# The inverse blocks of a chunked delta rule: U and T loaded together, the way out in two halves, and new orders of the steps

## The chip, the cores and the metric

One Trainium2 chip, of which the kernel uses one core. The metric is device time in microseconds (us) for one launch. Everything is float32. The names of the engines are those of the profile: PE is the matrix engine (PEld its loads of weights), DVE the vector engine, ACT the scalar engine, POOL the GpSimd engine, and SP the queue that issues nearly all transfers (DMAs).

## The reference, cut to what matters

A layer normalisation feeds two branches that are added to the input: a gated delta rule (linear attention with 32 heads of 64, 4 sequences of 256 tokens) and a small gated feed-forward part (1024 wide, with Walsh-Hadamard transforms). The change lies in the delta rule.

```
xn = layernorm(x)
q, k, v, z = split(xn @ w_qkvz.T)
q, k, v = causal depthwise convolution of 4 taps
g = -exp(A_log) * softplus(a + dt_bias); beta = sigmoid(b)
q = l2norm(q) / 8; k = l2norm(k)
for t in range(256):
    S = S * exp(g_t)
    delta = (v_t - k_t @ S) * beta_t
    S = S + outer(k_t, delta)
    o_t = q_t @ S
out = (rmsnorm(o) * norm_weight * sigmoid(z)) @ w_out.T
y = x + out + ffn(xn)
```

## The kernel before, in words

The loop over tokens is replaced by chunks of 64 tokens. Within a chunk the deltas solve a triangular system of 64 by 64, so the kernel forms the Gram matrix of the keys (gram, L779), scales it (ATP, L309), and inverts the triangle. A step of the kernel handles one pair of heads m (16 pairs, `PAIRS`), and for it 16 units (4 sequences by 4 chunks), with the two heads of a pair on the two halves of the 128 partitions.

The inverse is made in two stages.

- The base: the 4 diagonal blocks of 16 by 16 of each of the 32 triangles are carried to one row per block. `bout` (L641) writes the blocks of ATP to the DRAM scratch `base_blocks`, 8 DMAs of 16 KB; `bin_` (L647) reads them back as 128 rows of 256 numbers into `UU[:, 0]`; DVE inverts all 128 blocks at once in 16 small instructions (`inv` with i of 0, 1, 2, L338 to L360); ACT writes the transposed blocks into `UU[:, 1]` (L1090); `uout` (L653) writes both to the scratch `inverse_blocks`, and `uin` (L665 to L668) brings them back to where the matmuls want them: the blocks U to `U16` (8 DMAs), the transposed T to `T16` (6 DMAs), and the first block column to `X` (2 DMAs). Each of these 16 DMAs has 16 partitions by 16 units by 16 numbers, 16 KB.
- The rest of the triangle: `hz` on PE with j of 0 to 3 (L802, L804, L806), where ACT turns the first product into Q (L1099), and DVE adds U to the products (`hz` on DVE, L371).

Behind it stands the serial part of the pair, per chunk c: `delta` (L835, d copied by ACT at L1105), `state` (L848, added by DVE at L387), `ks` (L818, added by DVE at L376), then the outputs `o` (L863), their norm and gate, and `out` (L915, L421). Beside all this run the projections of later pairs (`proj`, L715 on PE, L1043 on ACT, L259 on DVE, the costliest lines), the norms of the keys (`stats`), the feed-forward part (`ff`, `fo`), and POOL's scalings.

Each engine works through a list of steps that is written out by hand as text ("0.hz.1.0" is pair 0, step hz, j of 1, half 0); the engines meet only in semaphores. An engine therefore waits at the head of its own list, whatever stands behind. On SP one list orders `load` (weights of the projection, 512 KB, L599), `rload` (decay rows, 6 DMAs, L614 and L617), `fload`, `oload` (128 KB, L632), `bout`, `bin`, `uout` and `uin`. `uout` waits for ACT's transposition (`ut_done`), `uin` for `uout` to land, and PE's `hz` of j 0 for all of `uin` (`ui_in` at 16 times `UIN`). `UIN` counts the DMAs.

```
uin waits: uu_out, then issues 16 DMAs (UIN = 16 * 16)
hz, j = 0, on PE: pe.wait_ge(ui_in, (m + 1) * UIN)
```

Of the kernel before, what the change touches and what calls it, by code (L numbers as in the profile page):

```python
# [89 lines left out]
def layer(nc, sem, sb, ps, k, cst, xnT, beta, yacc, xh, wdf, coef, x, wqkvz, wba, conv, alog, dtb, nw, wout,  # L90
          su_ug, su_dp, ws_up, ws_gate, ws_dp, wgu, wdown, consts, drows, dblk, dub):

    with ExitStack() as ctx:
# [153 lines left out]
        with nc.Block() as block:  # L247
            @block.vector
            def _(dve):
# [266 lines left out]
                for n in (15, 13, 11, 9, 7, 5, 3, 1):  # L516
# [20 lines left out]
                         "state": state, "norm": norm, "gated": gated, "turn": turn, "out": out, "fold": fold, "fo": fo}, """0.fold 0.proj.0 0.proj.1 0.proj.2 0.proj.3 0.e 0.proj.4 0.stats 0.proj.5 0.gram.0 0.gram.1 1.e 0.ff 0.gram.2 0.gram.3  # L537
                     1.proj.0 1.proj.1 0.fo.0 1.proj.2 1.proj.3 0.inv.0 1.proj.4 1.stats 1.proj.5 1.ff 1.gram.0 1.gram.1 0.inv.1 0.fo.1
                     0.inv.2 1.gram.2 1.gram.3 0.vtr.0 1.fo.0 2.ff 0.vtr.1 2.proj.0 2.e 1.fo.1 2.fo.0 3.ff 2.proj.1 2.fo.1 2.proj.2
                     0.hz.1.0 3.fo.0 0.hz.1.1 1.inv.0 0.hz.2.0 0.hz.2.1 3.fo.1 0.hz.3.0 0.hz.3.1 1.inv.1 2.proj.3 0.state.0 0.ks.1 2.proj.4  # L540
                     0.state.1 0.ks.2 0.norm.0 1.inv.2 0.state.2 0.gated.0 0.ks.3 2.stats 2.proj.5 0.norm.1 0.turn.0 2.gram.0 2.gram.1
                     0.gated.1 0.out.0 2.gram.2 0.turn.1 0.out.1 1.vtr.0 0.out.2 0.out.3 1.vtr.1 2.gram.3 3.proj.0 3.proj.1 3.e 1.hz.1.0
                     1.hz.1.1 2.inv.0 1.hz.2.0 1.hz.2.1 3.proj.2 1.hz.3.0 1.hz.3.1 3.proj.3 1.state.0 2.inv.1 1.ks.1 3.proj.4 1.state.1
                     1.ks.2 1.norm.0 2.inv.2 1.state.2 1.gated.0 1.ks.3 3.stats 3.proj.5 1.norm.1 1.turn.0 3.gram.0 3.gram.1 1.gated.1
                     1.out.0 1.turn.1 1.out.1 3.gram.2 3.gram.3 1.out.2 1.out.3 2.vtr.0 2.vtr.1 4.proj.0 4.proj.1 2.hz.1.0 2.hz.1.1
                     2.hz.2.0 2.hz.2.1 2.hz.3.0 2.hz.3.1 3.inv.0 4.e 2.state.0 3.inv.1 2.ks.1 4.proj.2 2.state.1 4.proj.3 2.ks.2 2.norm.0
                     4.proj.4 2.state.2 2.gated.0 2.ks.3 3.inv.2 2.turn.0 2.norm.1 4.proj.5 2.gated.1 2.out.0 2.turn.1 2.out.1 4.stats
                     3.vtr.0 2.out.2 4.gram.0 4.gram.1 2.out.3 4.ff 3.vtr.1 4.gram.2 3.hz.1.0 3.hz.1.1 4.gram.3 3.hz.2.0 3.hz.2.1 5.e
                     3.hz.3.0 3.hz.3.1 5.proj.0 5.proj.1 3.state.0 4.inv.0 3.ks.1 4.inv.1 3.state.1 5.proj.2 3.ks.2 3.norm.0 5.proj.3
                     3.gated.0 3.state.2 5.proj.4 3.ks.3 4.inv.2 3.turn.0 3.norm.1 5.proj.5 3.gated.1 3.out.0 3.turn.1 3.out.1 5.stats  # L550
                     4.vtr.0 5.gram.0 3.out.2 3.out.3 5.gram.1 5.ff 4.vtr.1 5.gram.2 5.gram.3 4.hz.1.0 4.hz.1.1 4.hz.2.0 4.hz.2.1 6.e
                     4.hz.3.0 4.hz.3.1 6.proj.0 6.proj.1 4.state.0 5.inv.0 4.ks.1 5.inv.1 4.state.1 6.proj.2 4.ks.2 6.proj.3 4.norm.0
                     4.state.2 6.proj.4 4.ks.3 4.gated.0 5.inv.2 4.turn.0 4.norm.1 6.proj.5 4.out.0 4.gated.1 4.turn.1 6.stats 5.vtr.0
                     6.gram.0 4.out.1 4.out.2 4.out.3 6.gram.1 6.ff 5.vtr.1 6.gram.2 5.hz.1.0 5.hz.1.1 6.gram.3 5.hz.2.0 5.hz.2.1 7.e
                     5.hz.3.0 5.hz.3.1 7.proj.0 7.proj.1 5.state.0 6.inv.0 5.ks.1 6.inv.1 5.state.1 7.proj.2 5.ks.2 5.norm.0 7.proj.3
                     5.gated.0 5.state.2 7.proj.4 5.ks.3 6.inv.2 5.turn.0 5.norm.1 7.proj.5 5.out.0 5.gated.1 5.turn.1 7.stats 6.vtr.0
                     7.gram.0 5.out.1 5.out.2 7.gram.1 5.out.3 7.ff 6.vtr.1 7.gram.2 7.gram.3 6.hz.1.0 6.hz.1.1 6.hz.2.0 6.hz.2.1 8.e
                     6.hz.3.0 6.hz.3.1 8.proj.0 8.proj.1 6.state.0 7.inv.0 6.ks.1 7.inv.1 6.state.1 8.proj.2 6.ks.2 6.norm.0 8.proj.3
                     6.state.2 8.proj.4 6.ks.3 6.gated.0 7.inv.2 6.turn.0 6.norm.1 8.proj.5 6.gated.1 6.turn.1 6.out.0 6.out.1 8.stats
                     7.vtr.0 6.out.2 8.gram.0 6.out.3 8.gram.1 7.vtr.1 8.ff 8.gram.2 8.gram.3 7.hz.1.0 7.hz.1.1 7.hz.2.0 7.hz.2.1 9.e  # L560
                     7.hz.3.0 7.hz.3.1 9.proj.0 9.proj.1 7.state.0 8.inv.0 7.ks.1 8.inv.1 7.state.1 9.proj.2 7.ks.2 9.proj.3 7.norm.0
                     7.state.2 9.proj.4 7.ks.3 7.gated.0 8.inv.2 7.turn.0 7.norm.1 9.proj.5 7.out.0 7.gated.1 7.turn.1 9.stats 8.vtr.0
                     9.gram.0 7.out.1 9.gram.1 7.out.2 7.out.3 9.ff 8.vtr.1 9.gram.2 9.gram.3 8.hz.1.0 8.hz.1.1 8.hz.2.0 8.hz.2.1 10.e
                     8.hz.3.0 8.hz.3.1 10.proj.0 10.proj.1 8.state.0 9.inv.0 8.ks.1 9.inv.1 8.state.1 10.proj.2 8.ks.2 10.proj.3 8.norm.0
                     8.state.2 10.proj.4 8.ks.3 8.gated.0 9.inv.2 8.turn.0 8.norm.1 10.proj.5 8.gated.1 8.out.0 8.turn.1 10.stats 10.gram.0
# [743 lines left out]
```

## Time and profile before

| | |
|---|---|
| median of 3 runs | 844.16 us (843.19 to 848.38) |
| the profiled execution's own time | 839.25 us |
| its span, first to last instruction | 837.5 us |
| outside the span | 1.75 us |
| granted PE clock, mean over the span | 0.974 of full |
| instructions in the span | 27042 |

The durations of the prediction come from the profiled execution, whose time lies 4.9 us under the median of the three runs. A busy share of an engine is its busy time over the span; matmuls are pipelined, so a busy PE need not be at its peak. A row of a timeline gives the start, the time it took (of all instructions merged into the row) and, in brackets, how long the engine was idle before it and who ended that.

### The profile page before, as it was taken

What the parts mean: (1) busy time and instruction counts of PE and PEld (TensorE: products, weight loads), DVE (VectorE), ACT (ScalarE), POOL (GpSimd) and SP (SyncE); (2) the same over time, 40 slices, a digit from 0 to 9 for tenths busy, and PEclk for the clock granted to TensorE, in tenths of its full rate; (3) what the DMA queues carried; (4) which work ended last, traced back from release to release, by engine and by line L of the source; (5) the groups of instructions that cost most, each with busy time, mean ns of one, the idle gap of its engine ahead of it and who ended that gap; (6) DMA issues with size and microseconds to landing.
All of it is one profiled execution on the core that took longest, in us unless ns stands there. A gap on an engine that the chain in (4) does not pass through costs nothing.

```text
span 837.5 us, 27042 instructions
## 1 busy us (share of the span) xinstructions
PE 743.5 (89%) x11562; PEld 490.0 (59%) x11562; DVE 688.2 (82%) x1224; ACT 326.3 (39%) x737; POOL 278.0 (33%) x186
## 2 busy tenths in 40 slices
PE   1869997989899989999999999999988898989986
PEld 1534554655666656755666566666565565656674
DVE  4688995988789879878989989898897888896645
ACT  2234432525353526343443535253634335353210
POOL 3025321605243241525133323426061523242301
PEclk9979998999999999999999999999999999999989
DMA  7122230321414050312314040413113140302201
...
DMA packets 131703, 49.28 MB, mean 59 GB/s; under 512 B 111488, under 2 KB 121088, under 8 KB 131456
## 3 DMA queue, kind: packets, MB, share of 16 engines
...
## 4 chain that ended last, share of the span: by engine, by line
PE 48%; DVE 15%; SPq 14%; DMA 10%; issue 7%; ACT 4%; POOL 2%; DVEq 0%; ACTq 0%; POOLq 0%
PE bank L715 15%; SPq L641 4%; PE bank L863 4%; PE bank L835 4%; SPq L665 4%; DVE kq L259 3%; DMA UU<-base_blocks 3%; PE bank L743 3%; PE bank L736 3%; SPq L667 3%; PE bank L806 3%; PE bank L915 2%; DMA inverse_blocks<-UU 2%; DMA base_blocks<-ATP 2%; PE bank L848 2%
## 5 line engine op out<-in xcount | busy, mean ns | idle before, releaser
L715 PE MATMUL bank<-xnT,wq 128*128 128x512 f32 x512 | 254.4, 622 | 1.3 <-DVE kq L259 1.1
L259 DVE SCALAR_TENSOR_TENSOR kq<-bank,cw,kq 128x510 f32<-128x510 f32 (+2 forms) x288 | 213.6, 745 | 17.9 <-ACT kq L1043 11.0
L715 PEld LDWEIGHTS bank<-xnT,wq 128*128 128x128 f32 x512 | 90.8, 194 | 83.4 <-issue 72.1
L1043 ACT ACTIVATE kq<-bank,cw 128x512 f32<-128x512 f32 x96 | 65.8, 687 | 174.8 <-PE bank L715 146.6
L1231 POOL TENSOR_TENSOR Sd<-St,dec 128x256 f32<-128x256 f32 x32 | 22.6, 706 | 276.5 <-DVE St L383 224.0
L1235 POOL TENSOR_TENSOR ost<-ost,cst 128x8 f32<-128x8 f32 x32 | 53.8, 1680 | 134.1 <-DVE ost L396 134.0
L1225 POOL TENSOR_TENSOR kqg<-kq,rows 128x1024 f32<-128x1024 f32 x32 | 77.4, 2438 | 41.9 <-DVE kq L259 41.9
L915 PE MATMUL bank<-wo,oT 128*128 128x256 f32 x256 | 68.2, 384 | 0.0
L1195 POOL TENSOR_TENSOR stat<-stat,cst 128x16 f32<-128x16 f32 x16 | 46.3, 2896 | 39.8 <-DVE nV L318 39.8
L736 PE MATMUL bank<-xh,wguT 128*128 128x512 f32 x128 | 57.9, 595 | 0.0
L371 DVE TENSOR_TENSOR X<-U,bank 128x256 f32<-128x256 f32 (+1 forms) x96 | 42.8, 460 | 17.9 <-PE bank L804 8.2
L915 PEld LDWEIGHTS bank<-wo,oT 128*128 128x128 f32 x256 | 45.8, 190 | 16.6 <-issue 10.8
L806 PE MATMUL bank<-X,Q 64*32 64x32 f32 x2048 | 41.4, 195 | 14.2 <-DVE X L371 10.4
L1105 ACT ACTIVATE d<-bank 128x256 f32<-128x256 f32 x64 | 24.5, 383 | 75.5 <-PE bank L835 75.3
L1074 ACT ACTIVATE vt<-bank 64x256 f32<-64x256 f32 x128 | 48.3, 377 | 9.6 <-PE bank L743 5.5
L806 PEld LDWEIGHTS bank<-X,Q 64*32 64x32 f32 x2048 | 36.6, 111 | 25.1 <-DVE X L371 14.3
L1203 POOL TENSOR_TENSOR gb<-E,stat 128x512 f32<-128x512 f32 x32 | 35.4, 1126 | 46.7 <-issue 27.1
L421 DVE TENSOR_TENSOR yacc<-yacc,bank 128x512 f32<-128x512 f32 x64 | 42.9, 680 | 9.7 <-PE bank L917 4.9
L1065 ACT ACTIVATE kc<-bank 64x256 f32<-64x256 f32 x128 | 48.2, 377 | 4.4 <-PE bank L743 1.2
L1047 ACT ACTIVATE zt<-bank 128x512 f32<-128x512 f32 x32 | 17.6, 595 | 75.7 <-DVE oT L409 69.0
L309 DVE TENSOR_TENSOR ATP<-bank,gb 128x512 f32<-128x512 f32 x64 | 42.4, 683 | 5.1 <-PE bank L779 2.9
L743 PE MATMUL bank<-cst,kq 128*128 128x128 f32 x256 | 41.0, 289 | 1.8 <-DVE ATP L309 1.8
...
## 6 DMA issues: line engine op xcount, KB each, us to landing
...
rows<-decay_rows SPq DMA_DIRECT2D x32, 256.0 KB, 4.3
inverse_blocks<-UU SPq DMA_DIRECT2D x16, 256.0 KB, 2.0
wguT<-wgu_dram SPq DMA_DIRECT2D x8, 256.0 KB, 4.1
...
base_blocks<-ATP SPq DMA_DIRECT2D x128, 16.0 KB, 1.8
...
```

The costliest lines, as they stand in the source:

```text
L259: nc.vector.scalar_tensor_tensor(out=y[:, :, t:S], in0=p[:, :, 0:S - t], scalar=cw[:, m, i // 2, 3 - t:4 - t], in1=y[:, :, t:S], op0=ALU.m ...
L715: last = nc.tensor.matmul(ring[i % 2][:], wq[:, q, kc, i // 2, :], xnT[:, kc, (i % 2) * 512:(i % 2) * 512 + 512], start=kc == 0, stop=kc = ...
L736: last = nc.tensor.matmul(ff_bank(m, j)[:], wguT[:, j, kc, :], xh[:, kc].rearrange("p (b t c) -> p b t c", b=B, t=2)[:, :, q, :], start=kc ...
L743: last = nc.tensor.transpose(TG[H][:, i * P:i * P + P], kq[:, which, 2 * H + i // 2, i % 2 * P:i % 2 * P + P], k("ident"))
L806: last = nc.tensor.matmul(M[H][top[h], i * n + n - H2:i * n + n], Q[hs[h], u, 0:H2], X[hs[h], q, u, H2:C], start=True, stop=True)
L915: last = nc.tensor.matmul(dst, oT[:, t, b, :], wo[:, q, :], start=True, stop=not ffn)
L1043: nc.scalar.activation(kq[:, i // 2, 2 * (i % 2):2 * (i % 2) + 2, :], split(ring[i % 2][:], 2), ACT.Copy, scale=cw[:, m, i // 2, 3:4]).the ...
L1065: nc.scalar.activation(kc_[place(h, H), H * HALF + c:H * HALF + HALF:2], split(TG[H][hs[c], :], 4)[:, :, h * C:h * C + C], ACT.Copy).then_ ...
L1074: nc.scalar.activation(vt[place(h, H), H * HALF + c:H * HALF + HALF:2], split(TG[H][hs[c], :], 4)[:, :, h * C:h * C + C], ACT.Copy).then_i ...
L1195: nc.gpsimd.tensor_tensor(stat[:, 2], stat[:, 5], k("half"), ALU.pow).then_inc(root_done, 1)
L1225: nc.gpsimd.tensor_tensor(kqg[:, q, :, half(H)].rearrange("p k u c -> p k (u c)"), src, g, ALU.mult).then_inc(kqg_done, 1)
L1235: nc.gpsimd.tensor_tensor(ost[:, 2, :], ost[:, 1, :], k("neghalf")[:, 0:B * 2], ALU.pow).then_inc(rms_done, 1)
```

## The change

U16 and T16 become the two halves of one tile `UT`, and `inverse_blocks` is laid out with the kind (U or T) ahead of the unit. Then one DMA brings a block of U and of T for all 16 units: 8 DMAs of 16 partitions by 32 by 16 numbers (32 KB) in place of 14 of 16 KB, with the 2 for X as they were, 10 DMAs for a pair in place of 16. The T block of the last block row, which before was not loaded, comes along. `uout` is issued as two DMAs of 128 KB: the half with U as soon as DVE has inverted (`inv_step`), the half with T when ACT has transposed. One memset on POOL in place of two. The lists of all five engines are written anew; the counts of steps in them are the same (657, 116, 755, 418 and 176 for DVE, SP, PE, ACT and POOL).

```
-        U16 = tmp("U16", [UNITS, C])
-        T16 = tmp("T16", [UNITS, C])
+        UT = tmp("UT", [2, UNITS, C])
+        U16, T16 = UT[:, 0], UT[:, 1]
...
-        UIN = 16 * 16
+        UIN = 16 * 10
...
                 def bin_(m, q):
                     sp.wait_ge(at_out, (m + 1) * 2 * NB * 16)
-                    wait(sp, uu_out, m * 16)
+                    wait(sp, uu_out, m * 32)
                     sp.dma_start(UU[:, 0], dblk.rearrange("h i u r c -> (h i u) (r c)")).then_inc(nb_in, 16)
                 def uout(m, q):
-                    sp.wait_ge(ut_done, m + 1)
                     wait(sp, ui_in, m * UIN)
-                    sp.dma_start(dub.rearrange("h i u k r c -> (h i u) (k r c)"), UU[:].rearrange("p k f -> p (k f)")).then_inc(uu_out, 16)
+                    sp.wait_ge(inv_step, (m + 1) * NINV)
+                    for i in range(2):
+                        if i:
+                            sp.wait_ge(ut_done, m + 1)
+                        sp.dma_start(dub[:, :, i].rearrange("h i u r c -> (h i) u (r c)"), UU[:, i]).then_inc(uu_out, 16)
                 def uin(m, q):
-                    sp.wait_ge(uu_out, (m + 1) * 16)
+                    sp.wait_ge(uu_out, (m + 1) * 32)
...
                     for h in range(2):
                         for i in range(NB):
                             at, cols = h * C + i * BASE, slice(i * BASE, i * BASE + BASE)
-                            sp.dma_start(U16[at:at + BASE, :, cols], dub[h, i, :, 0].rearrange("u r c -> r u c")).then_inc(ui_in, 16)
-                            if i < NB - 1:
-                                sp.dma_start(T16[at:at + BASE, :, cols], dub[h, i, :, 1].rearrange("u r c -> r u c")).then_inc(ui_in, 16)
-                        sp.dma_start(X[h * C:h * C + BASE, q, :, 0:BASE], dub[h, 0, :, 0].rearrange("u r c -> r u c")).then_inc(ui_in, 16)
+                            sp.dma_start(UT[at:at + BASE].rearrange("p k u c -> p (k u) c")[:, :, cols], dub[h, i].rearrange("k u r c -> r (k u) c")).then_inc(ui_in, 16)
+                        sp.dma_start(X[h * C:h * C + BASE, q, :, 0:BASE], dub[h, 0, 0].rearrange("u r c -> r u c")).then_inc(ui_in, 16)
...
-                ("inverse_blocks", (2, C // BASE, UNITS, 2, BASE, BASE)))]
+                ("inverse_blocks", (2, C // BASE, 2, UNITS, BASE, BASE)))]
```

Of the lists two lines, from DVE's:

```
-                     0.hz.1.0 3.fo.0 0.hz.1.1 1.inv.0 0.hz.2.0 0.hz.2.1 3.fo.1 0.hz.3.0 0.hz.3.1 1.inv.1 2.proj.3 0.state.0 0.ks.1 2.proj.4
+                     0.hz.1.1 3.fo.0 0.hz.2.0 0.hz.2.1 1.inv.0 3.fo.1 0.hz.3.0 0.hz.3.1 1.inv.1 2.proj.3 0.state.0 0.ks.1 2.proj.4
```

SP, from the second half of pair 0's loads of the inverse blocks to pair 1's way into UU. Before:

```order
L665 DMA U<-inverse_blocks 16x16x16
L667 DMA T<-inverse_blocks 16x16x16
L665 DMA U<-inverse_blocks 16x16x16
L668 DMA X<-inverse_blocks 16x16x16
L632 DMA woraw<-wout_dram 128x256
L641 DMA base_blocks<-ATP 16x16x16 x8
L599 DMA wq<-wqkvz_dram 128x1024
L647 DMA UU<-base_blocks 128x256
```

Now, from the way out of pair 0 on (L656 is `uout`, L668 the loads of UT, L669 those of X):

```order
L656 DMA inverse_blocks<-UU 8x16x256 x2
L632 DMA woraw<-wout_dram 128x256
L668 DMA UT<-inverse_blocks 16x32x16 x4
L669 DMA X<-inverse_blocks 16x16x16
L668 DMA UT<-inverse_blocks 16x32x16 x4
L669 DMA X<-inverse_blocks 16x16x16
L641 DMA base_blocks<-ATP 16x16x16 x8
L599 DMA wq<-wqkvz_dram 128x1024
L647 DMA UU<-base_blocks 128x256
```

A pair now has 10 of these loads and not 16, and the load of the output weights (L632) moved from behind them into the wait for the way out. The load of the projection's weights still stands ahead of L647.

DVE, in pair 0's `hz` (L371), where the base inverse of pair 1 begins (L338, which waits for L647's DMA). Before:

```order
L371 TENSOR_TENSOR X<-U,bank 128x8x48
L439 TENSOR_TENSOR yacc<-yacc,bank 128x2x256
L371 TENSOR_TENSOR X<-U,bank 128x8x48
L338 MEMSET UU 128x16
L340 TENSOR_TENSOR prod<-UU 128x8
L341 TENSOR_TENSOR UU<-UU,prod 128x4x2
L342 TENSOR_TENSOR prod<-UU 128x8
L343 TENSOR_TENSOR UU<-UU,prod 128x4x2
L371 TENSOR_TENSOR X<-U,bank 128x8x32 x2
L439 TENSOR_TENSOR yacc<-yacc,bank 128x2x256
L371 TENSOR_TENSOR X<-U,bank 128x8x32 x2
```

Now:

```order
L371 TENSOR_TENSOR X<-UT,bank 128x8x48 x2
L439 TENSOR_TENSOR yacc<-yacc,bank 128x2x256
L371 TENSOR_TENSOR X<-UT,bank 128x8x32 x2
L338 MEMSET UU 128x16
L340 TENSOR_TENSOR prod<-UU 128x8
L341 TENSOR_TENSOR UU<-UU,prod 128x4x2
L342 TENSOR_TENSOR prod<-UU 128x8
L343 TENSOR_TENSOR UU<-UU,prod 128x4x2
L439 TENSOR_TENSOR yacc<-yacc,bank 128x2x256
L371 TENSOR_TENSOR X<-UT,bank 128x8x32 x2
```

The first instruction of the base inverse, and the wait in front of it, moved from behind the two additions of j 1 to behind the two of j 2.

DVE, the same place in pair 11 (base inverse of pair 12). Before:

```order
L371 TENSOR_TENSOR X<-U,bank 128x8x48 x2
L371 TENSOR_TENSOR X<-U,bank 128x8x32
L338 MEMSET UU 128x16
L340 TENSOR_TENSOR prod<-UU 128x8
L341 TENSOR_TENSOR UU<-UU,prod 128x4x2
```

Now:

```order
L371 TENSOR_TENSOR X<-UT,bank 128x8x48 x2
L371 TENSOR_TENSOR X<-UT,bank 128x8x32 x4
L338 MEMSET UU 128x16
L340 TENSOR_TENSOR prod<-UU 128x8
L341 TENSOR_TENSOR UU<-UU,prod 128x4x2
```

Here it moved behind all six additions of the pair. In pairs 1 and 13 it moved as in pair 0, in pair 14 behind all six as in pair 11; in pairs 3 to 9 it stands in the same place in both lists, behind the first addition of `state`. On SP the 512 KB `load` of a later pair stands between `bout` and `bin` in pairs 1 and 6 before, and in pairs 0, 1, 4, 6, 7, 9, 10, 11, 12 and 13 now.

## Rows read from the trace of the kernel before

**Rows 1.** The page's busy time by engine (PE, DVE), and its last chain

```profile
PE 743.5 (89%) x11562; PEld 490.0 (59%) x11562; DVE 688.2 (82%) x1224; ACT 326.3 (39%) x737; POOL 278.0 (33%) x186
...
PE 48%; DVE 15%; SPq 14%; DMA 10%; issue 7%; ACT 4%; POOL 2%; DVEq 0%; ACTq 0%; POOLq 0%
```

**Rows 2.** Busy time by stretch: length, PE, PEld, DVE, ACT, POOL, clock, DMA share, GB/s

```profile
0.00:118.70 118.70, 85.81 (x522) 46.90 (x522) 93.64 (x149) 43.02 (x95) 35.46 (x24) 0.96 0.34 92
118.70:254.80 136.10, 120.00 (x2024) 80.00 (x2024) 110.66 (x205) 53.49 (x123) 45.31 (x30) 0.95 0.24 50
254.80:627.90 373.10, 356.63 (x5724) 235.84 (x5724) 327.47 (x583) 159.41 (x359) 135.29 (x90) 0.99 0.26 58
627.90:760.90 133.00, 117.23 (x2090) 79.97 (x2090) 113.53 (x208) 53.89 (x124) 50.09 (x34) 0.99 0.26 57
760.90:837.50 76.60, 63.84 (x1204) 47.26 (x1204) 42.86 (x85) 16.53 (x40) 11.84 (x9) 0.94 0.13 31
```

**Rows 3.** Who waited for whom: us in total, times, longest

```profile
DVE UU L338 <- DMA UU<-base_blocks: 18.7, 8, 5.5
...
PE bank L806 <- DVE X L371: 10.4, 7, 5.3
...
PE bank L802 <- DMA X<-inverse_blocks: 2.1, 4, 0.6
```

**Rows 4.** Timeline of SP, pair 0 to 1: start, us, instruction

```profile
109.18 0.33 SPq L665 DMA_DIRECT2D U<-inverse_blocks  x1
...
116.43 0.45 SPq L668 DMA_DIRECT2D X<-inverse_blocks  x1
...
117.46 6.61 SPq L641 DMA_DIRECT2D base_blocks<-ATP  x8
...
125.47 0.34 SPq L647 DMA_DIRECT2D UU<-base_blocks  x1
```

**Rows 5.** Timelines of DVE and PE at the same place

```profile
130.10 0.07 DVE L338 MEMSET UU<- 128x16 f32 x1 [5.49 <-DMA UU<-base_blocks]
...
124.87 1.20 PE L806 MATMUL bank<-X,Q 64*32 64x32 f32 x64
131.37 1.86 PE L806 MATMUL bank<-X,Q 64*32 64x32 f32 x62 [5.29 <-DVE X L371]
```

**Rows 6.** Stretches, columns as rows 2: behind the stall of pair 0, and two later ones

```profile
131.37:135.40 4.03, 4.03 (x67) 2.93 (x68) 3.19 (x10) 0.00 (x0) 0.00 (x0) 0.50 0.00 0
180.00:184.00 4.00, 3.98 (x38) 2.79 (x39) 3.16 (x6) 0.38 (x1) 0.62 (x1) 0.57 0.01 4
368.00:372.00 4.00, 3.92 (x83) 3.27 (x83) 3.49 (x9) 0.60 (x1) 1.62 (x2) 0.59 0.02 4
```

**Rows 7.** Timeline of SP: issues of DMAs with many rows

```profile
0.74 1.00 SPq L672 DMA_DIRECT2D xs<-x_dram  x2
1.79 0.89 SPq L674 DMA_DIRECT2D cst<-consts_dram  x1
...
17.76 0.43 SPq L685 DMA_DIRECT2D yacc<-x_dram  x1
```

**Rows 8.** One stretch of loads of the inverse blocks alone, columns as rows 2

```profile
480.00:488.00 8.00, 7.99 (x32) 5.29 (x31) 6.50 (x11) 1.77 (x3) 6.71 (x5) 1.00 0.31 30
```

**Rows 9.** Timelines of SP, DVE and PE, pair 11

```profile
626.57 5.15 SPq L641 DMA_DIRECT2D base_blocks<-ATP  x8
...
636.49 0.07 DVE L338 MEMSET UU<- 128x16 f32 x1 [3.12 <-DMA UU<-base_blocks]
...
642.73 0.68 PE L835 MATMUL bank<-nV,X 64*64 64x64 f32 x16 [2.23 <-issue]
```

**Rows 10.** Timeline of PE, pair 15: its first product with T

```profile
798.40 2.07 PE L802 MATMUL bank<-T,ATP 64*64 64x48 f32 x64
```

**Rows 11.** The page's DMA issues: count, KB each, us to landing

```profile
inverse_blocks<-UU SPq DMA_DIRECT2D x16, 256.0 KB, 2.0
```

**Rows 12.** The chain in order of time: `bin` behind a 512 KB load, and alone

```profile
361.04 4.43 DMA UU<-base_blocks
...
455.36 2.10 DMA UU<-base_blocks
```

More of the change, by code:

```diff
@@ L543, in _ @@
[L543 to L546, printed above, removed]
@@ L551, in _ @@
[L551 to L554, printed above, removed]
+                     0.gated.1 0.out.0 2.gram.2 0.turn.1 0.out.1 1.vtr.0 2.gram.3 0.out.2 1.vtr.1 0.out.3 3.proj.0 3.proj.1 1.hz.1.0 3.e
@@ new lines, in _ @@
+                program({"load": load, "rload": rload, "fload": fload, "oload": oload, "bout": bout, "bin": bin_, "uout": uout, "uin": uin}, """0.rload 1.rload 0.bout 2.load 0.bin 2.fload 2.rload 0.uout 1.oload 0.uin 1.bout 3.load 1.bin 1.uout 2.oload 1.uin
+                     3.rload 2.bout 2.bin 4.load 2.uout 2.uin 3.bout 4.rload 3.bin 4.fload 5.load 3.uout 3.uin 3.oload 5.rload 4.bout
+                     6.load 4.oload 4.bin 4.uout 4.uin 6.rload 5.bout 5.bin 6.fload 7.load 5.uout 5.oload 5.uin 7.rload 6.bout 8.load 6.bin
+                     6.uout 6.oload 6.uin 8.rload 7.bout 9.load 8.fload 7.bin 7.oload 7.uout 7.uin 9.rload 8.bout 8.bin 10.load 8.uout
+                     8.uin 8.oload 10.rload 9.bout 10.fload 11.load 9.bin 9.uout 9.uin 11.rload 10.bout 12.load 9.oload 10.bin 10.uout
+                     10.uin 12.rload 10.oload 11.bout 13.load 11.bin 11.oload 11.uout 11.uin 12.bout 14.load 12.bin 13.rload 12.oload
+                     12.uout 12.uin 13.bout 15.load 12.fload 13.bin 13.oload 14.rload 13.uout 13.uin 15.rload 14.bout 14.bin 14.oload
+                     14.uout 14.uin 15.bout 15.bin 15.oload 14.fload 15.uout 15.uin""")
@@ L968, in _ @@
                 program({"decays": decays, "proj": proj, "ff": ff, "ktr": ktr, "vtr": vtr, "qsq": qsq, "gram": gram, "hz": hz, "ks": ks, "delta": delta,
-                         "state": state, "o": o, "turn": turn, "out": out, "wd": wd, "fo": fo}, """0.proj.0 0.proj.1 0.decays 0.wd.0 0.proj.2 0.ktr.0 0.proj.3 0.wd.1 0.proj.4 0.ktr.1 0.proj.5 0.ff 0.gram.0 0.proj.6
-                     0.proj.7 0.gram.1 1.proj.0 0.fo.0 1.proj.1 0.vtr.0 0.vtr.1 1.proj.2 0.qsq 1.proj.3 1.ktr.0 0.fo.1 1.ktr.1 1.proj.4
@@ L991, in _ @@
-                     7.proj.5 5.ks.3 7.ktr.1 5.delta.3 5.turn.0 5.o.1.0 5.o.1.1 5.o.1.2 7.proj.6 5.out.0 7.gram.0 7.proj.7 5.turn.1 5.out.1
-                     5.out.2 7.ff 5.out.3 6.hz.0.0 6.hz.0.1 7.gram.1 6.hz.1.0 6.hz.1.1 6.hz.2.0 6.hz.2.1 8.proj.0 6.hz.3.0 6.hz.3.1
+                         "state": state, "o": o, "turn": turn, "out": out, "wd": wd, "fo": fo}, """0.decays 0.proj.0 0.proj.1 0.wd.0 0.proj.2 0.ktr.0 0.proj.3 0.wd.1 0.ktr.1 0.proj.4 0.proj.5 0.ff 0.proj.6 0.gram.0
+                     0.proj.7 0.gram.1 1.proj.0 0.vtr.0 0.fo.0 1.proj.1 0.qsq 1.proj.2 0.vtr.1 1.proj.3 1.ktr.0 0.fo.1 1.proj.4 1.ktr.1
@@ L1029, in _ @@
+                     13.fo.1 14.out.2 14.out.3 15.hz.0.0 15.hz.0.1 15.hz.1.0 15.hz.1.1 15.hz.2.0 15.hz.2.1 15.hz.3.0 15.hz.3.1 15.delta.0
+                     15.state.0 15.ks.1 15.delta.1 15.state.1 15.o.0.0 15.ks.2 15.o.0.1 15.o.0.2 15.delta.2 15.state.2 15.ff 15.ks.3
+                     15.delta.3 15.turn.0 15.o.1.0 15.o.1.1 15.o.1.2 14.fo.0 14.fo.1 15.out.0 15.fo.0 15.fo.1 15.turn.1 15.out.1 15.out.2
+                     15.out.3""")
             @block.scalar
@@ L1189, in _ @@
+                     15.delta.3 15.ff 15.norm.1""")
             @block.gpsimd
```

287 lines of the change are left out of this document (141 added, 146 removed).

## The prediction

> **What bounds the kernel now.** I read the page's busy times first, then the chain, then the stretches, the waits, and last the timelines of single pairs. PE is busy 89% of the span and DVE 82%, and the chain that ended last is 48% PE, 14% issues on SP and 10% DMAs [rows 1]. Averages hide where that holds. By stretches [rows 2], PE is idle for 32.9 us of the first 118.7 us (the prologue, in which PE has nothing to do), for 16.1 us of the stretch of pairs 0 to 2 (136.1 less 120.0), for 16.5 us of the 373 us of pairs 3 to 10 (so PE is 96% busy there), for 15.8 us of pairs 11 to 13, and for 12.8 us of the tail. The whole idle time of PE behind the prologue is 61 us, and half of it lies where only a third of the pairs are. In the middle nothing that is not PE work can give more than some 2 us a pair.
>
> What ends the idle times? PE waited for the loads of the inverse blocks only 2.1 us in total, four times [rows 3]. So the direct effect of faster loads, PE starting its first product sooner, is small in the old list. The larger item is indirect: DVE waited 18.7 us, 8 times, for the DMA into UU (base inverse of the next pair), and PE 10.4 us for DVE's additions to X [rows 3]. The two are one thing. In pair 0, SP issues the 16 loads from 109.18 to 116.88 us, only then the way out of pair 1's blocks (117.46), and the DMA into UU at 125.47 [rows 4]. DVE stands at the head of its list with the base inverse, between the additions of j 1 and those of j 2, and waits 5.49 us; PE, which needs these additions, waits 5.29 us [rows 5]. Behind it the granted clock is 0.50 for the next 4.03 us, the lower of its two levels (1.2 GHz, not 2.4), and after two later stalls 0.57 and 0.59 over 4 us [rows 6]. A stall of PE is thus paid twice. Pair 11 repeats it: bout issued at 626.57 right behind the loads, DVE idle for 3.12 us, PE for 2.23 us [rows 9].
>
> **The loads.** Six DMAs fewer for each pair. Sixteen issues take 7.7 us, 0.48 each [rows 4], so ten take 4.8: 2.9 us less on SP for each pair, if an issue costs the same with 512 pieces of 64 bytes as with 256. No row shows such a DMA. From below: two loads of 512 rows of 1 KB were issued in 1.00 us together, and one of 1024 rows in 0.43 [rows 7], so pieces cost SP nothing. From above: the load right behind those two took 0.89 [rows 7], as if the queue had been full, and then 512 pieces cost 0.98, the ten issues 8 x 0.97 + 2 x 0.48 = 8.7 us, 1.0 more than now. The DMA engines do not decide: they are 0.31 busy in a stretch of these loads [rows 8], that is 8.0 x 16 x 0.31 = 40 engine-us for some 4100 pieces, 9.7 ns each; the new loads have 4608 pieces, 45 engine-us, 2.8 us of all 16, in 4.8 us. I take the fixed cost, as nearer to most rows: 2.9 us less, and 0.1 more to land.
>
> The Trainium skill (DMA: Bandwidth & Descriptors, section Bandwidth, Measured) gives about 10.5 ns for a small packet and calls transfers under 64 KB dominated by descriptors. The measured 9.7 ns agrees. Read as a rule for the whole DMA it speaks against the change, since the bytes are the same and the descriptors 12% more: by it the loads would take no less than before and the term above would be nothing.
>
> **The way out.** One DMA of 256 KB lands 2.0 us after its issue [rows 11]. Now the half with T, 128 KB, is issued at the same point, behind ACT's transposition, and the other ahead. It lands no later than 2.0 and, smaller, perhaps 0.3 sooner; the second issue can cost 0.3. I take nothing, with 1 us to either side of it. The load of the output weights moves into this wait in pairs 0 and 1 and some later ones, which takes another 0.5 us from between loads and bout.
>
> The same page (section on why a DMA increments its semaphore by 16) says that a DMA runs on the largest number of engines up to 16 that divides the outer dimension of both sides. The DRAM side of a half now has 8 there: 8 engines, 16 KB each, as before with 16 and twice the bytes. By that the landing stays 2.0, or more if both halves share the 8 engines in flight. No row here shows a DMA on 8 engines.
>
> **The stalls.** Here the lists and SP's shorter queue work together. Pair 0: bout starts 2.9 + 0.5 = 3.4 us sooner, so UU lands 3.4 us sooner, and DVE's wait stands behind the additions of j 2, so that PE can go on with two products of j 3 (1.2 us each, [rows 5]) and the projection behind them. Of 5.3 us I take 4.8 as gone, and 2.0 for the clock, since 4.03 us at half speed hold 2.0 us of work at full [rows 6]. Together 6.8 us. What is late next is DVE's own list, 110.7 us busy of 136.1 [rows 2], so not at once. Pair 11: the wait now stands behind all six additions, and PE's 2.2 us go. The other six waits are 18.7 - 5.5 - 3.1 = 10.1 us of DVE. By pair 0 nearly all of such a wait can reach PE, by [rows 2] in the middle little does; I take a third, 3.4 us, and for the clock one of the two later dips, 4 - 4 x 0.58 = 1.7 us. Sum of the gains: 6.8 + 2.2 + 3.4 + 1.7 = 14.1 us.
>
> **What it gives back.** The 512 KB load now stands ahead of bin in eight more pairs. Behind such a load UU landed 4.43 us after its issue, alone after 2.10 [rows 12]: 2.3 us later. Where bin comes sooner by 3 us that is covered, but in pairs where bout waited for ATP and not for SP it is not. I take a quarter of 8 x 2.3 = 18.6 us, 4.6 us. In pairs 3 to 9 the first product with T stands at the same place in PE's list as before, so sooner data find PE at other work: nothing. In pair 15 PE came to it without idling [rows 10]: nothing in the tail. The list in the prologue puts the decays ahead of the first projections, where PE idles anyway; nothing, or 2 us either way for the clock.
>
> **Sum.** 839.25 (the profiled execution: span 837.5 and 1.75 around it) - 14.1 + 4.6 = 829.7, so 9.5 us less. The median of the runs lies 4.9 us above the profiled one; 844.16 - 9.5 = 834.7, and I round the half microsecond that the first wait of PE for loads may add: 834.0 us. The forecast's own range is 827 to 839: the gain from 5 to 17 us.
>
> **Rivals.** A: the gain is hidden. For it: PE in the middle is 96% busy, and its other waits (for d, for Y, for St) are serial steps of a pair that no load shortens; when the stall at DVE goes, the same work waits there. Against: the stall of pair 0 is larger than any of those. Then only pair 0's own 5.3 us come through, less the 4.6 given back, 0 to 4 us: 842.
>
> B: pieces cost SP as much as issues do. For it: 0.89 behind the two loads of 512 rows [rows 7]. Against: 0.43 for 1024 rows. The loads then take 1.0 us more in each pair, under lists that no longer have spare work there; before, the first product started within a microsecond of the landing (it waited 4 times). 16 x 1.0 less what little slack there is, with 2.3 us for bin in eight pairs against only half the gains: +16 + 4.6 - 7 = +13.6, near 857. It decides once an issue of 512 pieces takes more than about 0.75 us.
>
> C: the 512 KB load ahead of bin isn't covered. The full 18.6 us in place of 4.6: 844.2 - 14.1 + 18.6 = 848.6, and a half-speed dip behind each of four of them, 1.7 each: 855. For it: 4.43 against 2.10. Against: base inverses stand five or more DVE steps behind, and in pairs 11, 12 and 14 they moved further back. It decides when DVE waits more than 25 us in total for UU.
>
> **How the numbers follow.** Forecast 0.54, A 0.28, B 0.08, C 0.10. A measurement of this kernel tells about 1% (8.4 us, 835.7) from no change. Of the forecast's share I put 0.44 beyond that and 0.10 within; A is within; B and C together 0.14 slower and 0.04 within. So faster 0.44, same 0.42, slower 0.14. The range reaches from 823, all gains and more of the early idle time, to 851, half of the slow cases.
>
> **What would show it.** Right: issues of UT near 0.48 us, SP done with a pair's loads in about 5 us; no wait of PE for X over 2 us near 125 to 135 us, and a clock near 1.0 there; the stretch up to pair 3's first product shorter by 7 or more us; the sum of DVE's waits for UU under 12 us; the stretch of pairs 3 to 10 within 3 us of 373. Wrong: issues of 0.9 us (B); waits of DVE for UU above 20 us, each behind a 512 KB load (C); the first stretch no shorter (A); or the middle stretch changed by more than 5 us, which nothing above explains.

## The result, and the profile after

The changed kernel took 814.53 us (median of 4 runs, 812.68 to 817.35), the kernel before 845.19 us beside it (4 runs, 843.19 to 848.38): a ratio of 0.9637, 95% interval 0.9593 to 0.968. That is 31 us less, where 10 were forecast, and 8.5 us below the low end of the range. The direction was right, the size was not.

The profiled execution has a span of 815.2 us, 22.3 less than the 837.5 of before. The page's busy times and its last chain, to be set beside [rows 1]:

```profile
PE 742.0 (91%) x11562; PEld 485.2 (60%) x11562; DVE 694.7 (85%) x1224; ACT 326.5 (40%) x737; POOL 278.8 (34%) x185
...
PE 54%; DVE 30%; issue 7%; ACT 4%; POOL 3%; DMA 1%; SPq 1%; DVEq 0%; ACTq 0%; POOLq 0%
```

PE has 1.5 us less to do and DVE 6.5 more; of the 22.3 us, 20.8 are idle time of PE that went. SP and the DMAs held 24% of the chain before and hold 2% now, and DVE's share went from 15% to 30%. The stretches, cut at the first product of pairs 0, 3, 11 and 14 as in [rows 2], with the same columns, show where:

```profile
0.00:117.90 117.90, 87.21 (x522) 47.92 (x522) 94.58 (x149) 43.01 (x94) 32.67 (x23) 0.96 0.35 93
117.90:241.30 123.40, 115.30 (x2030) 76.74 (x2028) 111.73 (x203) 52.47 (x121) 45.14 (x31) 1.00 0.28 59
241.30:608.80 367.50, 355.18 (x5721) 232.90 (x5720) 332.12 (x583) 159.53 (x354) 138.19 (x90) 1.00 0.27 59
608.80:738.10 129.30, 118.71 (x2093) 79.58 (x2092) 112.73 (x208) 53.57 (x125) 49.92 (x33) 0.99 0.27 59
738.10:815.20 77.10, 65.64 (x1204) 48.08 (x1204) 43.49 (x85) 17.88 (x43) 12.88 (x10) 0.91 0.14 31
```

Against the five lengths of before the differences are -0.8, -12.7, -5.6, -3.7 and +0.5 us. More than half of the gain is in pairs 0 to 2, where PE's idle time fell from 16.1 to 8.1 us and the granted clock rose from 0.95 to 1.00. Behind the prologue PE idles for 42.5 us in all (8.1 + 12.3 + 10.6 + 11.5), 18.7 less than before. The waits of [rows 3], and one on SP:

```profile
DVE UU L338 <- DMA UU<-base_blocks: 0.3, 1, 0.3
...
PE bank L807 <- DVE X L371: 0.5, 2, 0.3
...
PE bank L803 <- DMA X<-inverse_blocks: 0.5, 1, 0.5
...
SPq L641 <- DVE ATP L309: 48.8, 11, 6.4
```

DVE's wait for UU, 18.7 us before, has gone but for 0.3 us, and with it PE's wait for the additions, 10.4 before and 0.5 now. The last row is the other side: SP stands at `bout` and waits for ATP in 11 pairs, so in 5 of 16 alone `bout` comes straight behind other work of SP. In the trace of before those were 8. SP was the late one, and is less so. SP's timeline at the place of [rows 4]:

```profile
105.46 1.33 SPq L656 DMA_DIRECT2D inverse_blocks<-UU  x2
106.83 0.46 SPq L632 DMA_DIRECT2D woraw<-wout_dram  x1
109.38 3.44 SPq L668 DMA_DIRECT2D UT<-inverse_blocks  x4
112.86 0.49 SPq L669 DMA_DIRECT2D X<-inverse_blocks  x1
113.39 2.03 SPq L668 DMA_DIRECT2D UT<-inverse_blocks  x4
115.46 0.49 SPq L669 DMA_DIRECT2D X<-inverse_blocks  x1
116.05 3.83 SPq L641 DMA_DIRECT2D base_blocks<-ATP  x8
...
121.28 0.33 SPq L647 DMA_DIRECT2D UU<-base_blocks  x1
```

The DMA into UU is issued at 121.28, not 125.47. That is 11.9 us behind the first load of the blocks (109.38), where it was 16.3 (109.18). DVE and PE at the place of [rows 5]:

```profile
125.09 0.07 DVE L338 MEMSET UU<- 128x16 f32 x1 [0.31 <-DMA UU<-base_blocks]
```

```profile
123.11 1.20 PE L807 MATMUL bank<-X,Q 64*32 64x32 f32 x64
124.24 1.13 PE L943 MATMUL bank<-wdf,hf 128*128 128x256 f32 x4
125.30 1.20 PE L807 MATMUL bank<-X,Q 64*32 64x32 f32 x64
126.43 1.98 PE L716 MATMUL bank<-xnT,wq 128*128 128x512 f32 x4
```

DVE waited 0.31 us for 5.49, and PE runs through where it stood for 5.29. From pair 0's first product to pair 1's it is 39.8 us, where it was 47.1 (I read these periods off PE's timeline, here and below). The window there, and the page's issues, beside [rows 6] and [rows 11]:

```profile
128.00:136.00 8.00, 7.37 (x153) 4.89 (x156) 6.58 (x14) 3.64 (x9) 0.80 (x2) 1.00 0.01 2
```

```profile
UT<-inverse_blocks SPq DMA_DIRECT2D x128, 32.0 KB, 2.4
```

The clock is 1.00 and not 0.50. A load of both kinds lands 2.4 us after its issue.

### The profile page after: what moved, and what is told of

Read it like the earlier page. It is cut to its first block, busy times and chain, and to the rows that moved or that the text cites. A ratio compares the mean times of both kernels' runs of the same rounds, so it can differ in the third digit from the quotient of the medians.

```text
span 815.2 us, 26961 instructions
## 1 busy us (share of the span) xinstructions
PE 742.0 (91%) x11562; PEld 485.2 (60%) x11562; DVE 694.7 (85%) x1224; ACT 326.5 (40%) x737; POOL 278.8 (34%) x185
## 4 chain that ended last, share of the span: by engine, by line
PE 54%; DVE 30%; issue 7%; ACT 4%; POOL 3%; DMA 1%; SPq 1%; DVEq 0%; ACTq 0%; POOLq 0%
PE bank L716 17%; DVE kq L259 11%; PE bank L737 4%; PE bank L807 4%; PE bank L916 4%; PE bank L836 3%; PE bank L803 3%; PE bank L864 3%; PE bank L805 3%; PE bank L744 2%; PE bank L767 2%; PE bank L849 2%; PE bank L819 1%; PE bank L943 1%; PE bank L780 1%
## 5 line engine op out<-in xcount | busy, mean ns | idle before, releaser
L1232 POOL TENSOR_TENSOR Sd<-St,dec 128x256 f32<-128x256 f32 x32 | 20.8, 649 | 268.4 <-DVE St L383 218.7
L371 DVE TENSOR_TENSOR X<-UT,bank 128x256 f32<-128x256 f32 (+1 forms) x96 | 43.4, 461 | 17.5 <-PE bank L807 9.6
L916 PEld LDWEIGHTS bank<-wo,oT 128*128 128x128 f32 x256 | 45.9, 190 | 17.2 <-issue 12.1
L1204 POOL TENSOR_TENSOR gb<-E,stat 128x512 f32<-128x512 f32 x32 | 37.2, 1180 | 38.3 <-issue 21.7
L1212 POOL TENSOR_TENSOR kd<-kc,stat 128x512 f32<-128x512 f32 x32 | 37.2, 1164 | 18.8 <-DVE stat L299 18.8
```

The source lines that it names most:

```text
L916: last = nc.tensor.matmul(dst, oT[:, t, b, :], wo[:, q, :], start=True, stop=not ffn)
```

## The experiments

The measured ratios are to the kernel before, run beside each on the same chip, in brackets the 95% interval. The experiments ran in four sets, in which the kernel before had medians from 842.15 to 847.49 us. So a difference of two medians from different sets can be off by some us; where it matters, the difference of the ratios, times 845 us, stands beside it. The edits are shortened, and a line in words stands for code.

**Transfers alone, and lists alone.** First, the changed kernel's transfers under the five old lists:

```diff
-UIN = 16 * 16
+UIN = 16 * 10
-for kind in U16, T16: one load of 256 pieces each
+sp.dma_start(UT[at:at + BASE].rearrange("p k u c -> p (k u) c")[:, :, cols], dub[h, i].rearrange("k u r c -> r (k u) c"))
 (PE, DVE, ACT, POOL and SP lists as before)
```

> The new transfers (UT in 8 loads, the way out in two halves) under the five old lists. Theory 1 (transfers and lists each give a part, the stalls of DVE in front of the base inverse being what both work on): UU lands 3 us sooner where SP went straight from the loads to the next way out, DVE's waits for UU fall from 18.7 to about 8 us, and the time falls by 8 to 14 us, near 833. Theory 2 (the lists give all, the transfers only change what PE does not wait for): within 3 us of before, near 844. Theory 3 (the transfers give all): near the changed kernel, 815 to 820.

825.37 us, 0.9773 [0.9713, 0.9833]: 22 us less (19 by the ratio), between the first theory's 833 and the third's 820. The wait for UU in its trace:

```profile
DVE UU L338 <- DMA UU<-base_blocks: 8.9, 6, 2.3
```

It halved without a move in any list. Then the reverse, old transfers under the five new lists:

```diff
-UIN = 16 * 10
+UIN = 16 * 16
 (16 loads and one way out for each pair as before; the five lists of the changed kernel)
```

> The old transfers (16 loads, one way out) under the five new lists. Theory 1: each first product with T comes about 3 us later than its list has it, so PE waits up to 3 us a pair for the loads (in the trace of before it was 2.1 us in all): slower than the changed kernel by 15 to 30 us, near 835 to 845. Theory 2: 815 to 820. Theory 3: near 844.

828.68 us, 0.9801 [0.9738, 0.9864]: 19 us less (17 by the ratio), between two of the theories. UU costs DVE 2.8 us here, but PE stands in front of the late loads instead:

```profile
DVE UU L338 <- DMA UU<-base_blocks: 2.8, 2, 1.6
...
PE bank L802 <- DMA X<-inverse_blocks: 3.7, 3, 2.6
...
PE bank L818 <- DVE St L383: 5.1, 4, 2.9
```

Each half alone gives about two thirds of the 31 us. The parts overlap if anything (22 + 19 = 41), though the intervals don't exclude a plain sum: 0.9773 x 0.9801 = 0.958, some 0.009 either way.

**The give-back.** In the changed kernel the 512 KB loads (and `fload` where it stood there) are put behind `bin` again in eight pairs:

```diff
-0.rload 1.rload 0.bout 2.load 0.bin 2.fload
+0.rload 1.rload 0.bout 0.bin 2.load 2.fload
...
-4.bout 6.load 4.oload 4.bin 4.uout
+4.bout 4.oload 4.bin 6.load 4.uout
```

> The changed kernel with SP's 512 KB loads (and the feed-forward weights with them) issued behind the way into UU and not ahead of it, in the eight pairs where the change had newly put them ahead. If the load ahead costs what the prediction put down (2.3 us later for UU, a quarter of it reaching the end, 4.6 us): 3 to 6 us less than the changed kernel, near 810. If it is covered (DVE waited 0.3 us for UU in the changed kernel): within 2 us of 815. If the load itself is then late for the projections: slower, with PE waiting for the weights.

814.79 us, 0.9675 [0.9591, 0.9759], the changed kernel's time. The interval alone is wide; the traces say why there is nothing to win. The load ahead does delay UU: from issue to landing it takes 3.0 us in the median in the changed kernel, 2.1 in this run. But DVE waits for UU only 0.3 us in the one and not at all in the other. So the 4.6 us that I had given back, and rival C, are covered here.

**The base inverse's place.** Old transfers and lists with `inv.0` of the next pair moved back as the new lists have it, in pairs 0, 1 and 13 behind the additions of j 2, in 11 and 14 (with `inv.1`) behind those of j 3; and later the same in pairs 0 and 1 only:

```diff
-0.hz.1.0 3.fo.0 0.hz.1.1 1.inv.0 0.hz.2.0 0.hz.2.1 3.fo.1
+0.hz.1.0 3.fo.0 0.hz.1.1 0.hz.2.0 0.hz.2.1 1.inv.0 3.fo.1
...
-1.hz.1.1 2.inv.0 1.hz.2.0 1.hz.2.1 3.proj.2
+1.hz.1.1 1.hz.2.0 1.hz.2.1 2.inv.0 3.proj.2
```

> The kernel before with one thing changed: in DVE's list the start of the base inverse stands as in the new list in pairs 0, 1, 11, 13 and 14 (behind the additions of j 2, or behind all of them). Theory 1: PE's waits for X at 131 and 640 us go, 4 to 8 us less, near 838. Theory 2 (the lists give all, and this is their main step): 10 us less or more. The rival that a wait only moves along: within 2 us of 844, with DVE's wait for UU as long as before and PE waiting at delta in place of X.

> The kernel before (old transfers, old lists) with the start of the base inverse moved only in pairs 0 and 1. If the early term holds without the new transfers: 5 to 8 us less than before, near 839. If it needs them (UU comes too late wherever DVE waits for it): within 3 us of before.

844.81 us, 0.9974 [0.9937, 1.0011] for five pairs, and 840.29 us, 1.0006 [0.9968, 1.0044] for two. Nothing, twice, though in the first the wait for UU fell to 5.9 us; its last pairs gave the gain back (pair 14 took 40.6 us, before 37.5). In the second, where the period of pair 0 is 42.0 us in the profile, UU still waits:

```profile
DVE UU L338 <- DMA UU<-base_blocks: 14.2, 8, 3.7
```

The reverse, in the changed kernel: `inv.0` back where the old lists had it, in pairs 0, 1, 11 and 13, then in pairs 0 and 1 only:

```diff
-0.hz.1.1 3.fo.0 0.hz.2.0 0.hz.2.1 1.inv.0 3.fo.1
+0.hz.1.1 1.inv.0 3.fo.0 0.hz.2.0 0.hz.2.1 3.fo.1
...
-11.hz.2.0 11.hz.2.1 11.hz.3.0 11.hz.3.1 12.inv.0 12.inv.1
+11.hz.2.0 12.inv.0 12.inv.1 11.hz.2.1 11.hz.3.0 11.hz.3.1
```

> The changed kernel with one thing undone: in DVE's list the start of the base inverse stands again where it stood before in pairs 0, 1, 11 and 13 (between the additions). Theory 1 (what the lists give is that DVE no longer stands in front of the UU of the next pair while PE needs its additions): 4 to 9 us slower than the changed kernel, near 821, with PE waiting for X in pairs 0 and 1. Rival (with the shorter loads UU is there in time wherever it stands): within 2 us of 815.

> The changed kernel with the start of the base inverse put back only in pairs 0 and 1. By the periods of the run with all four put back (pair 1 longer by 3.4 us, pair 11 by 5.6, pair 13 by 6.8) this should cost 2 to 5 us, near 818, the other 10 us lying in pairs 11 and 13. If the early pairs carry the loss: 824 or more.

828.83 us, 0.9829 [0.98, 0.9859], and 818.01 us, 0.972 [0.9669, 0.977]. By medians the four places are worth 14 us, where 4 to 9 were expected, and of them pairs 0 and 1 hold 3.5 and pairs 11 and 13 the other 11; by the ratios it is 16, 7 and 9. That the places matter is clear, how they share it is not. In the first of these traces, at pair 13, DVE and then PE:

```profile
714.60 0.07 DVE L338 MEMSET UU<- 128x16 f32 x1 [1.95 <-DMA UU<-base_blocks]
```

```profile
718.09 1.92 PE L807 MATMUL bank<-X,Q 64*32 64x32 f32 x64 [2.77 <-DVE X L371]
```

```profile
718.10:722.10 4.00, 4.00 (x85) 3.49 (x86) 2.56 (x9) 0.00 (x0) 0.00 (x0) 0.50 0.01 4
```

The stall of [rows 5, 6] over again, in a later pair: 1.95 us at DVE become 2.77 at PE, and the same products (64 records in the trace, two for each product) that took 1.20 us take 1.92, with a granted clock of 0.50, its 1.2 GHz level, over 4 us. In the changed kernel DVE reaches that instruction at 708.82 and doesn't wait.

**The same move under the new transfers and old lists**, in pairs 0, 1, 11 and 13; with three Gram steps moved as well; and in pairs 0 and 1 only (the edit as above):

```diff
-3.vtr.1 4.gram.2 3.hz.1.0 3.hz.1.1 4.gram.3 3.hz.2.0
+3.vtr.1 4.gram.2 4.gram.3 3.hz.1.0 3.hz.1.1 3.hz.2.0
```

> The new transfers and the old lists, with only the start of the base inverse moved as in the new list in pairs 0, 1, 11 and 13. Theory 1: most of what the lists give, 4 to 9 us less than the new transfers under the old lists (825), near 819. Rival (the lists' part is spread over many small moves): within 3 us of 825.

> As the run before, and the last scaling of the Gram matrix (step gram with n of 3) ahead of the additions in pairs 3, 5 and 9, as in the new list, so that the blocks of the next pair go out sooner. Theory 1: another 2 to 3 us less, from the period of pair 5 (48.7 us under the old lists, 46.2 under the new), near 816. Rival: no difference from the run before, since that period has another cause.

> The new transfers under the old lists, with the start of the base inverse moved only in pairs 0 and 1. With the move in 11 and 13 too it gave 824.0, 1.4 less than without, and the period of pair 11 grew from 45.9 to 50.0 us in the profile. If that period is what took the gain back: 4 us less than 825, near 820. If not: 823 to 825.

823.96 us, 0.9773 [0.9743, 0.9804]; 825.17 us, 0.9792 [0.976, 0.9823]; 819.38 us, 0.9681 [0.9636, 0.9726]. So under the new transfers the move in pairs 0 and 1 gives 6 us (825.37 to 819.38; 8 by the ratios), where under the old ones it gave none, and is all but the last 5 us of the whole change (4 by the ratios). The same move in pairs 11 and 13 costs 5 us here (8 by the ratios), in lists that are old elsewhere: pair 11 then takes 50.0 us, not 45.9. The Gram steps do nothing.

**The way out in one piece.** In the changed kernel, one DMA of 256 KB behind ACT's transposition, with the 8 joint loads kept, and for that the unit ahead of the kind again in `inverse_blocks` and in `UT`:

```diff
-for i in range(2):
-    if i:
-        sp.wait_ge(ut_done, m + 1)
-    sp.dma_start(dub[:, :, i]..., UU[:, i]).then_inc(uu_out, 16)
+sp.wait_ge(ut_done, m + 1)
+sp.dma_start(dub..., UU[:]...).then_inc(uu_out, 16)
```

> The changed kernel with the way out in one DMA of 256 KB behind ACT's transposition, as before, and with the 8 loads of both kinds (the unit stands ahead of the kind in the scratch and in the tile UT). If the halves are what helps: slower than the changed kernel by 2 us or more. If the half on the path costs more than the whole did (2.7 us from the end of the transposition to the first load in the trace of the changed kernel, 2.0 in that of before): 0 to 5 us less, near 812. Either way the first load follows the transposition by about 2.0 us.

815.5 us, 0.9674 [0.964, 0.9708]: no difference. At the same pair of each, the transposition and what SP did behind it, first in the changed kernel, then in one piece:

```profile
229.49 0.63 ACT L1091 ACTIVATE UU<-UU 128x256 f32<-128x256 f32 x1
```

```profile
228.94 1.82 SPq L656 DMA_DIRECT2D inverse_blocks<-UU  x2
232.78 1.92 SPq L668 DMA_DIRECT2D UT<-inverse_blocks  x4
```

```profile
227.58 0.63 ACT L1088 ACTIVATE UU<-UU 128x256 f32<-128x256 f32 x1
```

```profile
228.24 0.33 SPq L653 DMA_DIRECT2D inverse_blocks<-UU  x1
230.26 1.91 SPq L665 DMA_DIRECT2D UT<-inverse_blocks  x4
```

From the transposition's end to the first load it is 232.78 - 230.12 = 2.66 us with halves and 230.26 - 228.21 = 2.05 in one piece. The halves cost 0.6 us on a path that has at least that much room. One piece and the 512 KB loads behind `bin` together are no better either:

```diff
 (both edits above)
```

> The way out in one piece and the 512 KB loads behind the way into UU, together, on the changed kernel. Each alone gave no difference; if both are hidden, the two together stay within 2 us of 815; if they only lacked the other (UU sooner and blocks sooner), 3 us less or more.

816.23 us, 0.9644 [0.9599, 0.9689].

**SP's queue by itself.** In the changed kernel, six more loads of 16 KB for each pair, behind the loads of the inverse blocks, into a tile that nobody reads, with a semaphore of their own (its waits are not shown). The kernel does this work in addition:

```diff
+for i in range(6):
+    sp.dma_start(split(idle[0:BASE, i * 256:i * 256 + 256], UNITS), dub[0, i % NB, 0].rearrange("u r c -> r u c")).then_inc(idle_in, 16)
```

> The changed kernel with six loads of 16 KB more for each pair, right behind the ten of the inverse blocks and into a tile that nobody reads: SP is busy as long as before the change (some 2.9 us more a pair), while the blocks themselves arrive as early as in the changed kernel. If the transfers' gain comes over SP's queue (a sooner way into UU): near the new lists with the old transfers, 825 to 829. If it comes from the blocks being there sooner for PE: within 3 us of 815. Both together lie between.

831.47 us, 0.9824 [0.9777, 0.987]. The waits and one pair's row:

```profile
DVE UU L340 <- DMA UU<-base_blocks: 11.8, 5, 3.8
...
DVE E L283 <- DMA rows<-decay_rows: 7.7, 4, 3.0
...
PE bank L826 <- DVE St L385: 8.5, 6, 2.9
```

```profile
197.48 2.90 SPq L676 DMA_DIRECT2D idle<-inverse_blocks  x6
```

The 2.9 us that six issues take, put back on SP where nobody waits for their data, cost 17 us (16 by the ratios) and bring the wait for UU back. PE's wait for the blocks themselves is 0.4 us, 0.5 in the changed kernel. So what the joint loads gave they gave to the DMAs that stand behind them on SP (the way out of the next pair's blocks, UU, the decays), not to the products that read them. The extra loads also take the DMA engines' time. Pair 0 lets the two be told apart:

```profile
108.56 1.92 SPq L672 DMA_DIRECT2D UT<-inverse_blocks  x4
123.28 0.34 SPq L650 DMA_DIRECT2D UU<-base_blocks  x1
127.17 0.07 DVE L340 MEMSET UU<- 128x16 f32 x1 [3.08 <-DMA UU<-base_blocks]
```

The DMA into UU is issued 14.7 us behind the first load of the blocks, in the changed kernel 11.9 (109.38 to 121.28). DVE goes on 3.9 us behind that issue, there 3.8. So in this pair the delay is SP's and not the engines'. Over all pairs the median landing of UU is 3.5 us, there 3.0, so the engines, or what else is in flight, may hold a part. And the time is 2 to 3 us above that of the old transfers under the same lists (828.68 us), so the loss isn't SP's share of the gain to the us.

**What a stall costs.** In the kernel before, 11 more products that nobody reads, in pair 0 at the start of j 3, ahead of its wait for additions, to keep PE busy through its stall:

```diff
+if m == 0 and j == 3 and H == 0:
+    pe.wait_ge(conv_step, 2 * 18 + 6)
+    for i in range(11):
+        nc.tensor.matmul(ring[1][:], k("ident"), xnT[:, 0, 0:512], start=True, stop=True)
 pe.wait_ge(hz_done, m * 6 + 2 * (j - 2) + H + 1)
```

> The kernel before with 11 matmuls of 128 x 512 more, whose result nobody reads, put into PE's stall of pair 0 (5.3 us long, in front of the last products of hz). If a stall is paid twice, over the clock: the granted clock behind the place stays at 1.00 and the work that took 4 us at 0.50 takes 2, so the next pair's first product comes 1 to 2 us sooner and the time falls by as much, which is less than the spread of the runs, so that the profile must show it. If the clock has another cause: 0.5 there as before, and nothing gained, or a loss of up to 1 us for the matmuls.

846.21 us, 0.9985 [0.9945, 1.0025]. In its trace:

```profile
125.52 9.71 PE L798 MATMUL bank<-xnT,cst 128*128 128x512 f32 x22
135.16 1.20 PE L810 MATMUL bank<-X,Q 64*32 64x32 f32 x64
```

```profile
134.00:138.00 4.00, 4.00 (x71) 1.96 (x69) 1.87 (x7) 0.00 (x0) 0.00 (x0) 1.00 0.00 0
```

The filler ran on for 9.7 us, over a stall that was 5.3 before and shorter in this execution, so the pair took 49.4 us and the time says nothing of the price. What it does show: with no idle time ahead of them the products run at clock 1.00, 64 records in 1.20 us, where [rows 5, 6] have 62 in 1.86 at 0.50. The dip belongs to the stall, not to the place.

## Why the prediction was wrong in size, and where it was right

**The loads: right.** "2.9 us less on SP for each pair". The 128 joint loads:

```profile
L668 SPq DMA_DIRECT2D UT<-inverse_blocks x128: 307/486/2006, 109.4 to 767.3; - x128
```

The columns are minimum, median and maximum in ns: 0.486 us at 512 pieces; the same column has 0.448 in the trace of before at 256 (its 0.48 was the distance from one issue to the next). Rival B wanted 0.75 and falls. A pair's loads hold SP for 8.2 us in the mean of the 16 pairs before and for 5.7 now, each counted from its first issue to its last one's end: 2.5 us less. They land in 2.4 us, 0.4 more than the separate loads and not 0.1. The prediction called the bytes the same; they are not, since the T block of the last row comes along: 8 x 32 + 2 x 16 = 288 KB a pair for 256, 12% more, as with the pieces. The Trainium skill (DMA: Bandwidth & Descriptors, section Bandwidth, Measured) calls transfers under 64 KB dominated by descriptors, under a table for loads issued from GpSimd. The 0.4 us for twice the pieces lean that way; the issue, which decides here, doesn't.

**The way out: right as a sum.** Nothing, and the run in one piece says the same, by way of 0.6 us of slack.

**The stall of pair 0: right in the profile, in part by luck.** 6.8 us forecast, 47.1 - 39.8 = 7.3 came, with the clock at 1.00. SP's queue gave more than the 3.4 us of the sum. From the first load of the blocks to the DMA into UU it is 15.8 to 16.3 us in the four profiles with the old transfers and SP's old list (before, the filler's, both moves), and 10.4 to 11.9 in three with the new ones (the changed kernel, and `inv.0` put back in four pairs and in two): 4.8 less in the mean. The 1.4 us more lie mostly in `bout`, whose eight issues took 4.2 to 6.6 us in the four and 3.8 to 4.8 in the three. The luck is in the stall that was read: in the trace of before DVE went on 4.6 us behind the issue of the DMA into UU, in the other three 2.9 to 3.0, so some 1.7 of its 5.49 us belong to that execution. Wrong was also to book the stall as a gain of its own. By itself the move gives 1.0006 (two pairs, old transfers); with the joint loads it is worth 6 us (8 by the ratios), and in the complete new lists its removal costs 3.5 (7). What made the pair faster is the queue and the move together.

**Pair 11 and the six other waits: too small.** "I take a third, 3.4 us", with 2.2 for pair 11 and 1.7 for one dip of the clock. Of the eight waits for UU seven went whole and the first to 0.3 us. The idle time of PE behind the prologue fell by 18.7 us where 4.8 + 2.2 + 3.4 = 10.4 were summed, and this is the term that was mis-sized in the profile. By stretches it fell by 8.0, 4.2, 5.2 and 1.3 us (pairs 0 to 2, 3 to 10, 11 to 13, and the tail). Its busy time fell by 1.5 us in all, of which pairs 0 to 2, with the clock at 1.00 for 0.95, hold 120.0 - 115.3 = 4.7; the other stretches took some back, where 3.7 were forecast for the clock. With the 2.2 us less of idle time in the prologue that makes the 22.4 of the profile. That a wait of 2 us at the head of DVE's list reaches PE in full, and dips the clock, is shown at pair 13 of the run with `inv.0` put back.

**The middle: wrong.** "Sooner data find PE at other work: nothing", for pairs 3 to 9. The stretch of pairs 3 to 10 gave 5.6 us, 4.2 of them idle time, and the prediction had named 5 as what it couldn't explain. One of the eight waits for UU lay there, in the trace of before:

```profile
365.54 0.07 DVE L338 MEMSET UU<- 128x16 f32 x1 [2.05 <-DMA UU<-base_blocks]
```

The dip at 368 to 372 us of [rows 6] stands right behind it, and that pair's period went from 48.5 to 46.2 us: 2.3 of the 5.6. The argument had looked at where PE's product with T stands in the list, and not at DVE's wait. With the new transfers alone that wait is still there and the period is 48.7 us:

```profile
357.05 0.07 DVE L338 MEMSET UU<- 128x16 f32 x1 [2.27 <-DMA UU<-base_blocks]
```

Under the new lists with the old transfers it is gone, and the period is 46.2. So these 2.3 us are the lists', though the base inverse stands at the same place in them. The stretch as a whole goes the other way: 368.7 us with the new transfers under the old lists, 374.3 with the old ones under the new lists. That is one profile each, and the kernel before with the move in pairs 0 and 1 took 370.2, so that the other 3.3 us are the transfers' is likely and not shown. They have no single place.

**The give-back: wrong.** 4.6 us; the time shows nothing of it. UU does land later behind the 512 KB loads, 3.0 us for 2.1, but DVE doesn't come to it before.

**From the profile to the median: wrong, and as large a step.** "The median of the runs lies 4.9 us above the profiled one", and the same 9.5 us were taken from both. The profiles differ by 22 us and the medians by 31. The runs list a mean granted clock. In 47 of the 58 runs of the kernel before beside these experiments (those that the ratios use) it was 0.965 in the median (831.6 to 850.4 us), and the slower runs have the lower clock, with a correlation of -0.70 (-0.74 in all 58, and -0.61 to -0.76 within each of the four sets): the 9 runs at 0.970 and above have a median of 840.3 us, the 8 at 0.960 and below 848.0. A line through them falls by 6.5 us for each 0.01. The profiled execution of before had 0.974 and so was one with few dips, and by that line 6 us better than a typical one; the changed kernel's profiled execution, 817.35 us, was its slowest, 2.8 us above its median, with 0.983 in runs of 0.983 to 0.987. The two are the 9 us. The line accounts for the 6; for the 2.8, at a clock as in the other runs, nothing here does. Whether the dips make a run slow or the stalls make both, the correlation doesn't say.

There is one slip of sign, too: half a microsecond that a wait may add was taken off, 834.0 for 834.7.

Set together: the mechanism was the forecast's, and the steps that failed are sizes in its sum. The idle time that goes with the stalls was taken too small, above all in the term of a third of the other waits (18.7 us went for 10.4, 4.2 of them in the middle, which was put at nothing); the give-back was 4.6 us and is nothing; and 9 us lie between a profile in which before had been lucky and the median, a step that the sum carried over unchanged. Rival A, the hidden gain, holds for one part alone, the move without the transfers. Rival C falls with the run that put the loads back.

**What stays open.** The changed kernel is 5 us faster than new transfers, old lists and two moves (814.53 and 819.38; 0.9637 and 0.9681, with intervals that overlap); which of the small moves gives that was not tried. Nor is it settled why the base inverse behind j 3 in pair 11 helps in the new lists and lengthens that pair to 50 us in the old. No version beat the changed kernel.
